# A decoder layer on one core: the load of x is issued at head 11 instead of 15, and the statistics of the attention's sum are taken and combined one head later

## What is computed

```python
x = x + attn(layernorm(x))           # RoPE; per token, softmax over its own 16 heads x 16 heads
x = x + xattn(layernorm(x), ctx)     # 16 heads; every token against all 2048 context tokens
x = x + moe(layernorm(x))            # 8 experts, top 2 by sigmoid gate, and a shared expert
# xattn, per head: q, k, v are rounded to 127 steps, then
attn = softmax(q @ k.T); attn = round(attn / s) * s     # s = max over the row / 255
out = attn @ v
```

## Time and profile before

| | us |
|---|---|
| median of 3 runs (1064.81 to 1065.13) | 1064.87 |
| the profiled execution, its own time | 1068.14 |
| its span, first to last instruction | 1065.7 |
| DVE busy | 906.5 (85%) |
| POOL, ACT, PE busy | 746.9, 737.3, 722.0 |
| the queue of SP's DMAs, share of 16 engines | 81.5% |

### The profile page before, as it was taken

How to read it: one execution, slowest core, us unless ns; L and a number is a source line. 1 busy time by engine, 2 the same in 40 slices (tenths; PEclk the granted TensorE clock), 3 DMA queues, 4 the chain that set the end, 5 groups by cost and what they waited for, 6 DMA issues and landing times. The chain is left out here.

```text
span 1065.7 us, 21210 instructions
## 1 busy us (share of the span) xinstructions
PE 722.0 (68%) x7072; PEld 388.6 (36%) x7072; DVE 906.5 (85%) x1841; ACT 737.3 (69%) x989; POOL 746.9 (70%) x728
## 2 busy tenths in 40 slices
PE   6966647666675867675776758576667767675674
PEld 4543323333342524343332425243333324242333
DVE  3887769989888899989898989899888989999851
ACT  2644656868677776868686877778686868878742
POOL 6688987787786778787886868787878868730000
PEclk9975777888896978889897989888878979798965
DMA  6012767979698896979797999979697979999981
GB/s 225 1 40 70 133 119 140 186 115 192 128 176 147 150 173 127 187 114 198 120 194 144 160 168 146 190 121 188 129 179 115 192 150 169 172 167 182 162 161 25
DMA packets 574019, 156.01 MB, mean 146 GB/s; under 512 B 567252, under 2 KB 571863, under 8 KB 573527
## 3 DMA queue, kind: packets, MB, share of 16 engines
q1 hardware_dynamic: 573910, 154.67, 81.5%
HBM read 9.93 MB, written 2.10 MB: 11 GB/s over the span
## 5 line engine op out<-in xcount | busy, mean ns | idle before, releaser
L1135 DVE TENSOR_SCALAR_CACHE_REDUCE score<-ps_score,q_neg 128x1024 f32<-128x1024 f32 x512 | 636.2, 1277 | 17.2 <-PE ps_score L1459 15.9
L824 ACT ACTIVATE prob<-score,exp_bias 128x2048 uint16<-128x2048 f32 x256 | 512.1, 2001 | 61.4 <-DVE exp_bias L1145 58.5
L1459 PE MATMUL ps_score<-keys,queries 128*128 128x512 bf16 x1024 | 368.1, 450 | 255.4 <-DVE score L1135 248.7
L1459 PEld LDWEIGHTS ps_score<-keys,queries 128*128 128x128 bf16 x1024 | 72.2, 103 | 445.7 <-DVE score L1135 415.9
L527 POOL TENSOR_TENSOR product<-hs_exp,v_tok 128x1024 f32<-128x1024 f32 x64 | 149.4, 2347 | 31.0 <-ACT hs_exp L789 30.8
L534 POOL TENSOR_TENSOR product<-product 128x512 f32<-128x512 f32 x128 | 159.5, 1262 | 0.0
L527 POOL TENSOR_TENSOR product<-qk_rot 128x1024 f32<-128x1024 f32 x64 | 150.2, 2349 | 0.3 <-POOL qk_rot L520 0.2
L1489 PE MATMUL ps_pv<-prob_t,values 128*32 128x128 f16 x4096 | 74.2, 229 | 25.1 <-DMA prob_t<-prob 24.8
L545 POOL TENSOR_TENSOR product<-product 128x512 f32<-128x512 f32 x64 | 80.8, 1271 | 5.9 <-POOL product L534 5.9
L1489 PEld LDWEIGHTS ps_pv<-prob_t,values 128*32 128x32 f16 x4096 | 63.2, 101 | 55.2 <-issue 55.2
L466 POOL TENSOR_SCALAR var_eps<-mean_var 128x1 f32<-128x1 f32 x48 | 12.6, 262 | 90.2 <-DVE mean_var L1080 89.2
(11 more groups left out here) (124 smaller groups left out, 1112.2 us busy)
## 6 DMA issues: line engine op xcount, KB each, us to landing
prob_t<-prob SPq DMA_TRANSPOSE x256, 4.5
prob_t<-in_w SPq DMA_DIRECT2D x3, 1024.0 KB, 4.8
x_in<-in_x SPq DMA_DIRECT2D x16, 128.0 KB, 3.0
score<-in_cond_t SPq DMA_DIRECT2D x4, 512.0 KB, 6.3
out<-x_out SPq DMA_DIRECT2D x16, 128.0 KB, 2.7
w_qkv<-in_w_qkv SPq DMA_DIRECT2D x1, 768.0 KB, 4.4
early<-in_w_kv SPq DMA_DIRECT2D x1, 512.0 KB
w_s<-in_w_s SPq DMA_DIRECT2D x3, 128.0 KB
```

Source lines behind the costliest of these rows:

```text
L824: act.activation(prob[:, s, :].bitcast(U16), score[:, s, :], ACT.Exp, bias=exp_bias[:, s:s + 1], scale=-1.0, accum_out=prob_sum[:, t.par, ...
L1135: dve.tensor_scalar(score[:, s, HALF * i:HALF * i + HALF], ps_score[:, score_slot(t.count(H, h), i)].rearrange("p b k -> p (b k)"), q_neg[ ...
L1459: mm = pe.matmul(ps_score[:, score_slot(n, i), b, :], queries[:, t.par, h // 2, h % 2, :], keys[:, h // 2, k0:k0 + KEYS], start=True, stop ...
```

## The change

SP issues the load of x of tile t+3 at head 11, in front of the transpose of head 11. DVE takes the statistics of kind 1 at head 9 + late instead of 8 + late (with the wait for `ho_projected` in front of it), and combines them at head 10 + late instead of 9 + late. No instruction is added or removed; the streams of PE, ACT and POOL are the same as before.

```diff
@@ SP, body @@
-                    if (t + 3).exists() and h == 15:
+                    if (t + 3).exists() and h == 11:
                         load_x(t + 3)
                     if t.exists() and by_dma(h):
                         turn(h, t)
@@ DVE, body @@
-                    if n.exists() and h == 9 + late:
+                    if n.exists() and h == 10 + late:
                         ln_combine(1, n)
...
-                    if n.exists() and h == 8 + late:
+                    if n.exists() and h == 9 + late:
                         dve.wait_ge(ho_projected, n.count(1, 1))
                         ln_gather(1, one_bank(n)[:, 0:D], n)
```

## The result

The median of four runs is **1057.93 us** (1056.75 to 1059.05); before, beside it on the same chip, 1064.84 us (1062.73 to 1065.13, four runs). The ratio is 0.9939, with a 95% interval of 0.9922 to 0.9957. The change makes the kernel faster by 6.9 us where 19 were forecast. The profiled execution of after took 1056.75 us, its span is 1055.0 us (before: 1068.14 and 1065.7). What the rows promise is therefore more than the medians can show.

A forecast was written before the change was run, and what follows sets the result against it. DVE was taken to bound the kernel, with the DMA engines' 54.6 us a body close below. Load -36.5 and late statistics +17.5 sum to -19.0 us, from 1064.87 to 1046 us, range 1026 to 1060.

The forecast's parts named there:

- the third rival: Head 0: the earlier load delays the routed transpose, DVE loses up to 0.9 us in 14 bodies, 1058 us; chance 0.15.
- the exchange at head 9: Head 9: the wait for L1424 becomes one for the scores, a loss of 0.15 us a body.
- What bounds the kernel: DVE sets the pace, busy 53.16 of 58.10 us a body; the DMA engines are a second floor at 54.6.
- The load, -36.5: Load at head 11: 13 waits of 2.9 us at head 0 nearly all go, as body 14 shows; 36.5 us gained.
- POOL's chain: Head 0: the layer norm's chain over POOL follows the earlier statistics in time, with 0.45 us to spare.
- The cost on SP, put at nothing: Heads 10 and 11: the load's 0.93 us issue delays a transpose some 0.5 us, absorbed by SP's gaps; no cost.
- The second wait is replaced, not removed: Head 9: PE works in order, so DVE waits for head 9's scores until 485.8 instead of L1424 until 485.38.
- The rival of the full gain (1001): Second part: the wait for L1424 is simply gone, 27.4 us gained, 1001 us; chance 0.04.
- The stall at head 10, 1.1 us of wait: Second half of head 10: late ACT delays PE's gate products and the scores behind; DVE waits 1.1, body loses 1.25 us.
- the 0.17 for its absence: Rival at head 10: the second stall does not come, only 0.15 us a body lost, 1030 us; chance 0.17.
- the rival of PE at 1.2 GHz through head 8: Head 8: PE's low clock, seen in three bodies, becomes the rule; 11 more bodies cost 25 us, 1071; chance 0.07.
- The term 14 x 1.25 = 17.5 us for the second part: Late statistics: the stall at head 10 costs 1.25 us in each of 14 bodies, 17.5 us lost, nothing giving it back.

The follow-up runs named there:

- the quiet one: Load at head 11, statistics not late, PE's projection ahead of the first values, those behind head 9's first scores, against the kernel before: 1016.61 us; load at head 13: 1010.58.
- the values moved: Late statistics added to the version with load at head 11, projection ahead of the values and values behind head 9's first scores (1016.61 us): 1035.88 us.

## Why the prediction was right or wrong

The sign and the range held; the size did not (6.9 us for 19). That the range held is in part luck. Its upper end was drawn for the third rival, whose 1058 us the median of 1057.93 meets by chance: that rival put 12.5 us at head 0, where after has 2.7 us more than before, and the rest came from elsewhere.

In bodies 1 to 13 the sum has -36.5 + 13 x 1.25 = -20.3 us, and the ledger -12.1. Of the 8.1 us between them DVE's longer work is 5.2 (4.9 in the gate's steps, 43.7 to 48.6), the second half of head 0 is 2.7 and the second half of head 10 is 2.5 (16.8 for 13 x 1.1). Some 2 us went the other way: the load's wait went whole, and the exchange at head 9 cost 0.9 us instead of 2.

- **What bounds the kernel.** Right. Both waits fell as each half was aimed, and DVE stayed the pace.
- **The load, -36.5.** The wait went whole (37.4 in the ledger), head 0 behaved as body 14 did, and POOL's chain was in time. As a run it was worth 32.5 us on the medians, 4 less, but 37.0 on the spans. The term was read from an execution that lies 3.3 us above its median, which is most of the difference. In bodies 1 to 13 the load alone gave 33.5 us: 37.4 less 2.0 at head 0 (2.5 for 0.5), 1.7 in the gate's steps and 0.4 at L1424, with some tenths of smaller items against them; the stretches around them gave 3.5 more.
- **The cost on SP, put at nothing.** Wrong by a little. The gaps behind the transposes of heads 10 and 11 did not absorb it all: 3.2 us of waits at the second half of head 0 against 0.5. The third rival (0.15) was right in its mechanism and too high in its price (12.5 us). The 0.93 us of its issue is not what DVE loses, since in eight of bodies 1 to 13 there is no wait. The rule of the Trainium skill named there (SBUF — State Buffer, "Can I just issue two DMAs to hit both halves?") has all transfers on the same 16 engines, one behind the other. The prediction made of it that the bytes of x are paid for wherever they are put, and the runs do not bear that out: with the load at head 13 the waits at head 0 went, from 3.2 to 0 us in the changed kernel and from 8.6 to 0.3 in the quiet one.
- **The second wait is replaced, not removed.** Right to a few tenths: 25.7 for L1424 became 26.6 for the first scores of head 9. The rival of the full gain (1001) fell with it.
- **The stall at head 10, 1.1 us of wait.** Right as a mechanism, against the 0.17 for its absence, and the run with PE's gate products behind the scores showed which link it is. Its size was right only where PE's clock stayed high: I took PE's durations from rows at full clock. There the wait is 0.80, below my 1.1, and two of those bodies last 56.56 us against my 56.5. In six of the bodies 2 to 13 the clock behind the stall is at 1.2 GHz or falls to it, and the wait is 1.6 to 2.1 us. Over the 13 bodies the waits add up to 16.8 us. It is not the rival of PE at 1.2 GHz through head 8: the waits above 3 us at head 9 stayed at three bodies, as in the earlier trace rows.
- **The term 14 x 1.25 = 17.5 us for the second part, with "I find nothing that gives this back".** This is the failed step: the runs have 26.9 us for it (26.3 on the spans). The term counted the waits of DVE, priced the stall at PE's full clock, took the durations of DVE's own instructions as fixed and let only bodies 1 to 14 pay. The gate's three steps, which the change moves in time against POOL's products, grew from 45.2 to 50.1 us (46.9 with the load alone). Ahead of body 1 the late statistics cost 1.8 us, where DVE's wait for POOL's L567 grows from 10.3 to 11.9 us, so it seems that there POOL did not have the idle time that the prediction gave it. Behind body 13 they cost 3.1 us, of which body 14 has 1.8, for the 1.25 that the term had there.

Of the 21.5 us that the second part costs in bodies 1 to 13 with the load in place, where the term had 16.3, head 10 has 16.8, the gate's steps 3.2, the second half of head 0 has 0.7 and the exchange at head 9 0.5. It stays open why the clock falls in some bodies and not in others: no run tried that by itself. On the medians the second part costs 32.5 us alone, 26.9 with the load and 19.3 with the values moved. In bodies 1 to 13 of the profiled executions the three are close together (18.2, 21.5 and 19.3 us), and the spans differ by 22.8, 26.3 and 23.6. So these runs do not show that its price depends much on the rest of the order.

## What to carry to other kernels

When a statistic or a copy is taken later to avoid a wait, follow the engine that is in order behind it: here ACT's next copy fed PE, and PE's order put that ahead of the scores which DVE wanted. The better cure for a wait on a late product was to move the product ahead in PE's stream (with the load of this change 47 us below the kernel before, of which 32.5 are the load's and some 14 come from the moves in PE's stream), not its reader back. And look at the duration of small instructions on the pacing engine: one of 8 elements that takes 2 us is a wait that no list of waits shows.

## What the runs showed of the hardware

DVE's gate steps L1167, L1169 and L1180 take 0.17 to 0.20 us when POOL is idle or its instructions are small, and up to 2.3 us beside a POOL product of 2.35 us, ending with it. The steps MAX8 and MATCH_REPLACE8 between them stay at 0.17 and 0.15 us in either case, and the big score steps at 1.28. The first run that shrank POOL's work made the delay smaller (from some 3.7 to 2.3 us a body), the second took it away (0.5). The Trainium skill has the mechanism, SBUF — State Buffer: VectorE and GpSimd share a port pair under an exclusive lock, held for the whole instruction, which a DVE operation wants in a two-port performance mode, or with two inputs in SBUF against a GpSimd operation that reads SBUF. The rows agree for these three steps, at a price of up to a whole POOL instruction for 8 elements. L1169 and L1180 have two inputs in SBUF and L1167 has one; which of the two conditions holds for which step was not tried.

Behind one and the same idle stretch of PE (1.62 us) the granted clock stayed high in six of the bodies 2 to 13 and fell to 0.50 in six, in three of them at once. DVE's wait went from 0.8 to 1.6 or 2.14 us with it.
